# A gated delta-rule layer with mixture-of-experts: the inverse's 16x16 diagonal blocks by substitution on GpSimd, in one more pipeline stage

## The reference

```python
q, k, v = short_conv(x @ Wq.T), short_conv(x @ Wk.T), short_conv(x @ Wv.T)   # 4 taps, silu; x is layer-normed
q, k = scale**2 * rmsn(q), scale * rmsn(k)
g = -exp(A_log) * softplus(x @ Wfa.T @ Wfb.T + dt_bias)       # one decay per channel and token
beta = sigmoid(x @ Wb.T)
def step(S, (q_t, k_t, v_t, g_t, b_t)):                       # over 512 tokens, per sequence and head
    S = S * exp(g_t)[..., None]
    delta = b_t * (v_t - k_t @ S)
    S = S + outer(k_t, delta)
    return S, q_t @ S
out = rmsn(o) * o_norm_w * sigmoid(x @ Wga.T @ Wgb.T) @ Wo.T
```

## Time and profile before

| | |
|---|---|
| median of 3 runs | 6376.87 us (6365.69 to 6393.16) |
| the profiled execution | 6372.03 us, of which 6370.3 us is the span of its instructions |
| PE / DVE / ACT / POOL busy | 93% / 65% / 51% / 32% of the span |
| mean granted clock of TensorE | 0.991 of 2.4 GHz |
| matmuls (PE) | 38912 (each fp32 product of two tiles counts twice, a transpose once) |
| mean DMA traffic | 18 GB/s |

### The profile page before, as it was taken

How to read it: one execution, slowest core, us unless ns; L and a number is a source line. 1 busy time by engine, 2 the same in 40 slices (tenths; PEclk the granted TensorE clock), 3 DMA queues, 4 the chain that set the end, 5 groups by cost and what they waited for, 6 DMA issues and landing times.

```text
span 6370.3 us, 128595 instructions
## 1 busy us (share of the span) xinstructions
PE 5917.3 (93%) x38912; PEld 4849.9 (76%) x38912; DVE 4167.3 (65%) x10433; ACT 3223.1 (51%) x6704; POOL 2018.3 (32%) x2752
## 2 busy tenths in 40 slices
PE   7999999999999999999999999999999999899999
PEld 5887777878787777777787878787777778755555
DVE  5766666666666666666676666667666666555555
ACT  4555555555555555555555555555555555411111
POOL 3333333333333333333333333333333333200000
PEclk9999999999999999999999999999999999999999
DMA  2000000000000000000000000000000000000000
GB/s 74 18 17 14 18 18 14 17 18 17 15 18 18 17 14 18 17 15 18 17 17 15 18 14 18 18 17 17 15 18 17 14 18 16 26 11 10 10 10 14
DMA packets 55174, 112.22 MB, mean 18 GB/s; under 512 B 5088, under 2 KB 38112, under 8 KB 54496
## 3 DMA queue, kind: packets, MB, share of 16 engines
q1 hardware_dynamic: 54624, 105.42, 5.3%
HBM read 97.01 MB, written 8.39 MB: 17 GB/s over the span
## 4 chain that ended last, share of the span: by engine, by line
issue 37%; PE 35%; POOL 18%; ACT 7%; DVE 2%; POOLq 1%; DVEq 0%; ACTq 0%
POOL kl L314 8%; PE bank L1133 8%; PE bank L1088 6%; PE bank L938 5%; PE bank L1105 3%; PE bank L1143 3%; POOL T L329 3%; POOL e_sb L340 3%; POOL e_sb L343 3%; ACT L512 2%; POOL TT L333 2%; PE bank L956 2%; PE bank L983 2%; ACT vs L442 2%; PE bank L968 1%
## 5 line engine op out<-in xcount | busy, mean ns | idle before, releaser
L314 POOL TENSOR_TENSOR kl<-kl,tot 128x256 f32<-128x256 f32 x768 | 503.6, 656 | 1787.0 <-PE bank L938 1773.4
L938 PE MATMUL bank<-kq,kl 128*128 128x128 f32 x6144 | 858.7, 283 | 75.6 <-DVE AT L637 53.0
L938 PEld LDWEIGHTS bank<-kq,kl 128*128 128x128 f32 x6144 | 752.6, 192 | 122.0 <-issue 74.6
L978 PEld LDWEIGHTS bank<-lx,TT 128*128 128x128 f32 x5120 | 630.6, 191 | 195.3 <-ACT lx L416 134.6
L956 PE MATMUL bank<-T,lx 128*128 128x64 f32 x6144 | 772.3, 268 | 0.0
L921 PE MATMUL bank<-xT,par 128*128 128x512 f32 x1536 | 766.8, 595 | 0.8 <-ACT gaT L397 0.8
L956 PEld LDWEIGHTS bank<-T,lx 128*128 128x128 f32 x6144 | 748.2, 192 | 0.0
L978 PE MATMUL bank<-lx,TT 128*128 128x64 f32 x5120 | 681.0, 276 | 55.4 <-ACT lx L416 35.9
L968 PE MATMUL bank<-ident,T 128*128 128x128 f32 x3072 | 482.5, 280 | 159.7 <-DVE T L659 159.7
L429 ACT ACTIVATE TT<-bank 128x256 f32<-128x256 f32 x768 | 295.8, 385 | 551.4 <-PE bank L968 550.0
L434 ACT ACTIVATE W<-bank 128x128 f32<-128x128 f32 x512 | 142.1, 278 | 784.4 <-PE bank L1019 784.4
(11 more groups left out here) (165 smaller groups left out, 12826.4 us busy)
## 6 DMA issues: line engine op xcount, KB each, us to landing
par<-params_dram SPq DMA_DIRECT2D x128, 519.0 KB, 3.5
wo<-wo_dram SPq DMA_DIRECT2D x128, 128.0 KB, 2.0
xall<-x_dram SPq DMA_DIRECT2D x16, 512.0 KB, 3.9
out_dram<-xall SPq DMA_DIRECT2D x16, 512.0 KB, 2.9
lx<-ffn_dram SPq DMA_DIRECT2D x1, 3456.0 KB, 11.7
wfa_sb<-wfa_dram SPq DMA_DIRECT2D x1, 128.0 KB, 2.2
wga_sb<-wga_dram SPq DMA_DIRECT2D x1, 128.0 KB, 2.0
wb_sb<-wb_dram SPq DMA_DIRECT2D x1, 8.0 KB, 2.0
```

What stands on the lines that cost most here:

```text
L314: pool.tensor_tensor(halves(kl[:, :], h)[:, :, 0, :], src, totr.broadcast_to([P, SEQ // (2 * h), h]), ALU.mult).then_inc(s["kl_ready"], 1)
L938: ins = pe.matmul(dst[:, :, n], chunk(left, n), right[:, :, n, :, 1, :], start=True, stop=True)
L978: ins = pe.matmul(b_x[:, 256 + n * HALF:256 + (n + 1) * HALF], chunk(TT[pB], n), XS[:, n * HALF:(n + 1) * HALF], start=True, stop=True)
```

## The change

The levels 0 to 3 no longer build T by matmuls. `l_evict` gathers their products, by predicated copies, in one tile `lt16` of the 16x16 diagonal blocks. ACT scales it by `sc` (`lt16_scale`, slot 4 of B). SP writes it to DRAM (256 KB), and four DMAs read the diagonal blocks back in pieces of 64 bytes, one block per partition, into `pm` (32 partitions by 256). POOL inverts all 32 blocks at once by substitution, 15 columns of two operations (`eliminate`), columns 0 to 9 behind `kl_update(6)` of step i, columns 10 to 14 behind `kl_update(0)` of step i+1. Four DMAs write the result `rm` to a second DRAM buffer, zero elsewhere, and one reads it back whole into `vd`. ACT scales `vd` into T (`t16_scale`), PE turns T (`turn_16`), ACT evicts all of TT (`tt16_evict`), and levels 4 to 6 go as before. They form a new stage D of head i-2; stage C is now of head i-3 (LAG = 3), so that kq, AT, sg, sc and eo have four buffers.

`supersteps` now writes out all eight heads of a sequence: one loop over the sequences, no loop over pairs. Wo is loaded once, whole (1 MB), behind the pieces of x, and PE waits for it before its first instruction. The expert weights also wait for the last output projection. Masks are 64 columns wide and are read with a step of zero over the chunks; `ident` has one chunk. `nsc`, the T and TT starts, line 948 and line 651 are gone.

The core of the diff:

```diff
+LOW, BLK = 4, 16
+HIGH = LEVELS - LOW
+NBLK = P // BLK
+LAG = 3
+def right_halves(ap, h):
+    return ap.rearrange("p (n m two h) -> p n m two h", n=NCH, two=2, h=h)[:, :, :, 1, :]
+def each_chunk(mask, h):
+    return mask.rearrange("p (m h) -> p m h", h=h).unsqueeze(1).broadcast_to([P, NCH, HALF // h, h])
...
+            def steps(b, heads, nb=None):
+                for h in heads:
+                    i = b * HEADS + h
+                    known = isinstance(i, int)
+                    A, B, D, C = [not known or 0 <= i - n < NHEAD for n in (0, 1, 2, LAG)]
+                    step(i, h, h % 2, b, bc, A, B, D, C, nb)
             batch_stage(0)
+            steps(0, range(HEADS - 2))
             with eng.Fori(1, BATCH) as b:
+                steps(b - 1, range(HEADS - 2, HEADS), b)
                 batch_stage(b)
+                steps(b, range(HEADS - 2))
+            steps(BATCH - 1, range(HEADS - 2, HEADS))
+            steps(BATCH, range(LAG))
...
# SyncE
+            sp.dma_start(wo_sb[:, :].rearrange("p (h d) -> p h d", d=HID), wo.rearrange("h p d -> p h d")
+                         ).then_inc(s["wo_in"], 16)
+                if D:
+                    sp.wait_ge(s["v_done"], iD + 1)
+                    for n in range(NCH):
+                        sp.dma_start(diagonal_of(blocks_in, n), blocks(rm, n)).then_inc(s["v_out"], 16)
+                    sp.wait_ge(s["v_out"], 16 * NCH * (iD + 1))
+                    sp.dma_start(vd, rows_of(blocks_in)).then_inc(s["v_in"], 16)
+                if B:
+                    sp.wait_ge(s["lt16_ok"], iB + 1)
+                    sp.dma_start(rows_of(blocks_out), lt16).then_inc(s["low_out"], 16)
+                    sp.wait_ge(s["low_out"], 16 * (iB + 1))
+                    for n in range(NCH):
+                        sp.dma_start(blocks(pm, n), diagonal_of(blocks_out, n)).then_inc(s["low_in"], 16)
+                    sp.wait_ge(s["low_in"], 16 * NCH * (iB + 1))
...
+            sp.wait_ge(s["out_mm"], 2 * NHEAD)
             sp.dma_start(lx[:, 0:(EXPERTS + 1) * 3 * HID], ffn_w).then_inc(s["f_w"], 16)
...
# GpSimd
+                def eliminate(iv, columns):
+                    each = 2 * (BLK - 1)
+                    rows = rm[:, :].rearrange("p (i c) -> p i c", c=BLK)
+                    for j in columns:
+                        if j == 0:
+                            after(pool, s["v_out"], 16 * NCH * iv)
+                            pool.tensor_tensor(rm[:, :], eye16[:, :], eye16[:, :], ALU.mult).then_inc(s["sub_step"], 1)
+                            pool.wait_ge(s["low_in"], 16 * NCH * (iv + 1))
+                        n, m = BLK - 1 - j, j + 1
+                        prod = mul16[:, 0:n * m].rearrange("p (i c) -> p i c", c=m)
+                        pool.wait_ge(s["sub_step"], each * iv + 2 * j + 1)
+                        pool.tensor_tensor(prod, pm[...].unsqueeze(2).broadcast_to([NB16, n, m]),
+                                           rm[...].unsqueeze(1).broadcast_to([NB16, n, m]), ALU.mult
+                                           ).then_inc(s["sub_step"], 1)
+                        pool.wait_ge(s["sub_step"], each * iv + 2 * j + 2)
+                        pool.tensor_tensor(rows[:, j + 1:BLK, 0:m], rows[:, j + 1:BLK, 0:m], prod, ALU.subtract
+                                           ).then_inc(s["sub_step" if j < BLK - 2 else "v_done"], 1)
                 if B:
                     kl_update(0)
-                    pool.tensor_tensor(T[:, :]..., eye, diag, ALU.mult).then_inc(s["t_init"], 1)
-                    pool.tensor_tensor(TT[pB][:, :]..., eye, diag, ALU.mult).then_inc(s["tt_init"], 1)
+                if D:
+                    eliminate(iD, range(10, BLK - 1))
+                if B:
                     for l in range(1, 5):
                         kl_update(l)
...
                 if B:
                     kl_update(6)
+                    eliminate(iB, range(0, 10))
...
# ScalarE
+                def lt16_scale():
+                    act.wait_ge(s["low_done"], LOW * (iB + 1))
+                    for n in range(NCH):
+                        ins = act.activation(chunk(lt16, n), chunk(lt16, n), ACT.Copy, scale=sc[mB][:, n:n + 1])
+                    ins.then_inc(s["lt16_ok"], 1)
+                def t16_scale():
+                    act.wait_ge(s["v_in"], 16 * (iD + 1))
+                    for n in range(NCH):
+                        ins = act.activation(chunk(T, n), chunk(vd, n), ACT.Copy, scale=sc[mD][:, n:n + 1])
+                    ins.then_inc(s["t16_ok"], 1)
+                def tt16_evict():
+                    act.wait_ge(s["t16_mm"], iD + 1)
+                    act.activation(TT[p][:, :], b_y[:, :], ACT.Copy).then_inc(s["tt16_ev"], 1)
+                    if slot == 4 and B:
+                        lt16_scale()
+                    if slot == 4 and D:
+                        t16_scale()
+                        tt16_evict()
+                        x_evict(4)
...
# VectorE
+                    if l < LOW:
+                        if l == 0:
+                            after(dve, s["low_out"], 16 * iB)
+                        dve.copy_predicated(right_halves(lt16, w), each_chunk(mask[l][:, :].bitcast(U32), w), right
+                                            ).then_inc(s["low_done"], 1)
                         return
-                    if B and slot == 1:
-                        t_update(0)
-                    if B and slot >= 2:
-                        t_update(slot - 1)
+                    if D and slot in (4, 5, 6):
+                        t_update(slot)
...
# TensorE
+            pe.wait_ge(s["wo_in"], 16)
+                def turn_16():
+                    pe.wait_ge(s["t16_ok"], iD + 1)
+                    for n in range(NCH):
+                        ins = pe.transpose(chunk(b_y, n), chunk(T, n), ident[:, :])
+                    ins.then_inc(s["t16_mm"], 1)
-                    if B and slot >= 2:
-                        turn_t(slot - 2)
-                    if B and slot >= 1:
-                        lt_times_t(slot - 1)
+                    if D and slot == 4:
+                        turn_16()
+                    if D and slot in (5, 6):
+                        turn_t(slot - 1)
+                    if D and slot in (4, 5, 6):
+                        lt_times_t(slot)
-                    if B and slot >= 2:
-                        t_products(slot - 1)
+                    if D and slot in (4, 5, 6):
+                        t_products(slot)
```

More of the change, by code:

```diff
@@ L76, in delta_moe @@
         par = [sb(f"par{p}", [P, PAR]) for p in range(2)]
-        wo_h = [sb(f"wo{p}", [P, HID]) for p in range(2)]
+        wo_sb = sb("wo_sb", [P, HEADS * HID])
         onw_sb = sb("onw_sb", [P, 1])
@@ L87, in delta_moe @@
         minus_half = sb("minus_half", [P, NCH])
-        mask = [sb(f"mask{l}", [P, NCH * HALF]) for l in range(LEVELS)]
+        mask = [sb(f"mask{l}", [P, HALF]) for l in range(LEVELS)]
         lower = sb("lower", [P, EXPERTS * EXPERTS])
@@ L109, in delta_moe @@
         xTs = [[chunk(xT, t, SEQ) for t in range(KT)], v]
-        sg = [sb(f"sg{p}", [P, SEQ]) for p in range(2)]
+        sg = [sb(f"sg{p}", [P, SEQ]) for p in range(4)]
         tk = [sb(f"tk{p}", [P, 8]) for p in range(2)]
@@ new lines, in _, with step @@
+            sp.wait_ge(s["scr_zero"], 16)
+            def step(i, h, p, bt, bc, A, B, D, C, nb):
+                iB, iD = i - 1, i - 2
+                if B and not (isinstance(i, int) and i + 1 >= NHEAD):
+                    for done, value in (("g_mm", i), ("conv_done", 3 * i), ("f_read", i), ("decay_done", i)):
+                        sp.wait_ge(s[done], value)
+                        sp.sem_inc(s["sp_go"], 1)
+                    sp.dma_start(par[1 - p][:, :], params[(h + 1) % HEADS]).then_inc(par_in[1 - p], 16)
+                if D:
+                    sp.wait_ge(s["v_done"], iD + 1)
@@ L481, in step @@
                         act.activation(ogT[:, :], b_k[:, :], ACT.Copy, scale=onw_sb[:, 0:1]).then_inc(s["ogt_ev"], 1)
-                    if B and slot >= 2 and not (A and slot in (5, 6)):
-                        tt_evict(slot - 2)
-                        x_evict(slot - 1)
+                    if slot == 4 and B:
[4 more added lines that the diff above has]
+                        x_evict(4)
+                    if D and slot in (5, 6) and not A:
+                        tt_evict(slot - 1)
+                        x_evict(slot)
                     if 1 <= slot <= 3 and C:
@@ L910, in batch_stage, with step @@
                     ins.then_inc(s[done], 1)
-            def step(i, j, p, bt, bc, ha, hc, A, B, C, nb):
-                iB, iC, pB = i - 1, i - 2, 1 - p
+            def step(i, h, p, bt, bc, A, B, D, C, nb):
+                iB, iC, iD, pB = i - 1, i - LAG, i - 2, 1 - p
+                m4, mB, mD, mC = [(h - n) % 4 for n in (0, 1, 2, LAG)]
+                j = bt * (HEADS // 2) + h // 2
+                hc = (h - LAG) % HEADS
```

410 lines of the change are left out of this document (188 added, 222 removed).

## The result

The changed kernel takes 6184.88 us (median of 4 runs, 6178.35 to 6196.64), against 6382.45 for the kernel before in the same comparison. The ratio is 0.9695, with a 95% interval of 0.9672 to 0.9718: 3% faster. The forecast was 6090, its range 5900 to 6350. The profiled execution took 6183.2 us, with a span of 6181.5 and a mean granted clock of 0.949.

What follows compares the result with a forecast made beforehand. PE is nearly full, but order, not work alone, sets the step. 127 steps save 41.34 - 37.5 - 1.0 = 2.8 us: 356. 6372.0 - 356 + 48 + 18 + 7 = 6089, say 6090; range 5900 to 6350.

Steps and rivals of the forecast that it cites:

- The clock's term: Sums and output projection behind PE's wait for the sigmoid: half clock costs 1.0 us per step, bounds 0 and 1.7.
- the ends: Paid once: +48 us at the start for Wo; at the end +18 for the drain, +7 for the expert weights.
- Steps 1 to 4: Level 0 to decay a, slots 1 to 4: gains of 0.75, 0.9 and 1.65 us, a loss of 0.4.
- The 0.75 of slot 1: DVE no longer does level 0's four T updates ahead of the first convolution: gain 0.75 us per step.
- Step 5: Slots 5 and 6, decay a to the sums: matmuls and evictions stay, nothing changes, 8.6 us.
- Step 6: Sums to level 0: level 6's t_products move ahead of the sums into PE's wait for ACT, gain 0.9 us.
- the rival of a clock that holds: Sums behind PE's wait: no fall to half clock, total 5963 us; chance 0.17.
- The rival of a second fall in the slots 3 and 4: PE's waits there drop the clock twice per step: step 40.9 us, total 6394, no change; chance 0.08.
- The drain: One more stage at the end: 23 us less 5 for quicker last levels, +18 us.
- The rivals of POOL: POOL's substitution in eliminate becomes the bound: at 0.62 us per operation, step 45.8, total 7017; chance 0.11.
- the 64-byte pieces: Block DMAs come late and ACT or POOL pays: 5 us too late gives about 6700; chance 0.04.
- The 8.6 us per head: PE work that leaves with the transpose, lt_times_t, turn and t_products groups: 1100 us in all.

Runs made afterwards that it cites:

- experiment 4: The changed kernel with level 6's last products behind the sums again and twelve dummy products in PE's wait for the sigmoid: 6092.95 us.
- Four products: The changed kernel with four extra 128x128 products per step, whose result nobody reads, in PE's wait for the sigmoid: 6013.31 us.
- experiment 6: The changed kernel with 4 of 30 substitution operations kept: 6129.64 us; with each substitution product computed twice: 6557.68 us. Also shows rows with four dummy products.
- the best version: The changed kernel with key transposes between three and three dummy products in the sigmoid wait, Wo loaded early, expert weights' wait moved later: 5900.95 us.

## Why the prediction was right, and where it was off

The sign, the mechanism and the range held. The number was 95 us too low. The clock's term carries some 53 of that, the ordinary steps some 30, the ends 13. These misses have one sign, so it wasn't errors cancelling that kept the number in the range.

**Steps 1 to 4, level 0 to a.** The prediction's terms make 27.04 - 2.9 = 24.14; measured 24.20 in the step shown, 24.40 in the mean of the ordinary ones. The 0.75 of slot 1 shows as the first convolution beginning 6.68 us behind level 0, where it stood 7.36 behind it. K·S started 9.28 behind it, where 9.0 was laid out. The two scalings took 1.27 and 1.26 instead of 1.15. The single terms weren't tried one by one; their sum is what is shown.

**Step 5**, a to sums: 8.6 forecast, 8.67 measured. **Step 6**: sums to level 0 fell from 5.69 to 4.84 at full clock, forecast 0.9 less; experiment 4 shows that term by itself (0.84). Together 37.5 forecast and 37.55 found in the better steps, once the clock holds; the mean of the ordinary ones is 37.9.

**The clock's term failed in size.** "I take 1.0 us per step, a little above the middle of the bounds 0 and 1.7." Four products take 40.70 - 39.28 = 1.42 us off the mean step. Of 74 ordinary steps 9 had no half clock, 45 had 3.4 us of it (sums to level 0 6.19), 20 had 6.8 us (7.29). So a fall costs up to 7.29 - 4.84 = 2.4 us: the upper bound was read from the one row of such a gap, whose stretch was a short one. The place and the cause were right. With the clock held the kernel takes 6013, where the rival of a clock that holds had 5963; the 50 us are the other misses below. The rival of a second fall in the slots 3 and 4 didn't come: level 0 to a is what it was without. The Trainium skill, "TensorE: Matmul & The Clock Gate", section "HAM oscillation — how this bites in real kernels", has a loop whose compute is shorter than its waits fall on every iteration. This loop isn't of that kind, with PE busy 86% and a wait of 2 us, and it kept the clock in 9 of 74 ordinary steps. The prediction gave that rule some 90 us more, which would be 6180. That this lies near the 6184.88 is luck: the clock's term itself measured 1.42, between the 1.0 taken and the rule's 1.7, and the rest of the 95 us came from other terms.

**The other steps, and an overlap that was left out.** I let the loop's end and `batch_stage` cost what they did, and they do: before, the 45 steps that they touch stand 45.27 - 41.34 = 3.93 us above an ordinary one; with four products, where nearly no half clock is left, 41.46 - 37.55 = 3.91. But the mean of the ordinary steps there is 37.95 and not 37.55. That is 0.4 in 74 of 119 steps, 0.25 per mean step, and most of it stands in the 35 steps in which DVE's update of `kq` is stretched beside POOL's `kl_update(0)` (experiment 6). The prediction named the hindrance and called `kl_update(0)` hardly late, but its sum had nothing for what DVE loses. With 0.42 from the clock and 0.05 from the step itself that makes the 0.7 us between the 2.84 forecast and the 273.7/127 = 2.16 found. It is worth 82 us over the 127 steps, against the rounded 356 of the sum.

**The ends.** Start: +48 forecast, 48.9 measured, first matmul 71 and 71.28. End: 18 + 7 = 25 forecast, 36.8 measured. The expert weights' part is near: PE waits 11.02 us for them instead of 5.56 for DVE, 5.5 for 7. The drain isn't: 31 for 18. PE's timeline of the drain in the changed kernel shows why.

```profile
5313.17 1.11 PE L1019 MATMUL bank<-ident,T 128*128 128x128 f32 x4 [3.45 <-ACT T L484]
5314.07 1.80 PE L1033 MATMUL bank<-T,lx 128*128 128x64 f32 x8
...
5331.28 3.78 PE L1188 MATMUL bank<-wo_sb,lx 128*128 128x256 f32 x8 [0.78 <-ACT lx L560]
```

The step of levels 0 to 6 is 5.5 us quicker than before, as laid out. The additional step takes 34.5 us where 23 were laid out. T's first part is ready after 12.8 us (11.8 forecast). With nothing beside them, the three last levels run at half clock, 1.80 us for what takes 1.00 in a full step, and take 16.3 for 11.4. And the turn of og and the output projection of the head before, 5.4 us at half clock, stand behind them in PE's order; the sum had no term for these. The last step of all is 2.4 us longer, with more of it at half clock.

**What had to stay hidden did.** Substitution: 11.0 us forecast, about 12.05 found. An operation took 0.294 + 0.076 = 0.37 (0.342 forecast), and the start of `rm` 0.95 instead of 0.6. It cost nothing, since the slack was 2 and not 1. The transfers: the three rows of SP's queue in the same step, and the medians to landing.

```profile
2507.54 1.37 SPq L261 DMA_DIRECT2D blocks_in<-rm  x4
2510.26 0.34 SPq L267 DMA_DIRECT2D lx<-blocks_in  x1
2519.09 0.34 SPq L272 DMA_DIRECT2D blocks_out<-lx  x1
```

```profile
blocks_out<-lx SPq DMA_DIRECT2D x128, 256.0 KB, 2.0
lx<-blocks_in SPq DMA_DIRECT2D x128, 256.0 KB, 2.7
```

The blocks are back 2.7 us behind 2510.26, at 11.2 in the step (12.4 forecast), and ACT wants them at 2518.90: 5.9 us of room. No wait of POOL ends on a DMA, and of ACT's only one, 2.9 us in the drain. The rivals of POOL and of the 64-byte pieces fell, the first with less room than any other: 0.06 us more per operation would have made it true.

**A mark that was wrong.** I looked for PE busy near 4800 us; it was 5292, and 5212 with four products, 140 us of them dummies. The 8.6 us per head were sums of groups that overlap their neighbours by some 0.15 us, ten groups per head, so that 190 us of them were counted twice. Half clock and single groups behind a wait lengthen the rest. This is argued from the rows and wasn't tried; the step's sum doesn't rest on it.

## What to carry to other kernels

When work is taken off an engine that is nearly full, look at what gap opens and what stands behind it: here the gap itself cost nothing (a to sums stayed at 8.6 to 8.7), the half clock that followed it cost 1.4 us per step, and a few products that nobody reads won back nearly as much (172 us) as the change itself had gained (198). Lay out a step by its stretches between named events, not by busy time, and let the clock's term run up to its full bound when full work follows the gap. Load a tensor where it is first needed: one wait ahead of the first instruction cost 57 us here, a fifth of what the best version gains over the changed one.

## What the runs showed of the hardware that wasn't expected

- One wait of 2.01 us, in a step in which PE is otherwise nearly always busy, was followed by half clock in 65 of 74 ordinary steps. Four products of 0.28 us each ended this in all 74, and with one product 53 still had it. More isn't better: with eight the fall behind the loop's end came in 14 of 15 instances, with four in 5.
- A GpSimd operation on 32 partitions hardly depends on its columns: 0.20 us for 15 and 0.28 for 64 when nothing else runs, with 0.08 between dependent ones. The first one behind `kl_update(0)`, beside DVE's work, took 0.72 (32x55), against 0.27 for the same shape later.
- The hindrance goes both ways. DVE's predicated copy of L takes 0.74 us beside POOL and 0.42 alone, in one step:

```profile
2503.04 0.74 DVE L695 COPY_PREDICATED lx<-mask,bank 128x256 f32<-128x256 uint32 x1 [0.40 <-PE bank L1011]
...
2510.89 0.42 DVE L695 COPY_PREDICATED lx<-mask,bank 128x256 f32<-128x256 uint32 x1
```

- The Trainium skill, "GPSIMD Engine Reference", section "Specifications", names the SBUF interface that the two engines share, and contention with DVE instructions that have two SBUF inputs. The updates of `kq` and `kl` in experiment 6 (0.72 or 1.55 us, 0.83 or 1.23) agree with it, in both directions. The predicated copy slows down too, though one of its two inputs, the product, comes from the bank.
